# Half of the softmax tiles leave TensorE's transposes for the DMA queue, and the normalisation moves from the tiles to the sums

## The reference

```
g     = x·w_g + b_g          theta = x·w_theta + b_theta      phi = x·w_phi + b_phi
att   = softmax(theta phi, axis=-1)          # 1024 x 1024 for each image
y     = att g                                # 1024 x 64
out   = x + batchnorm(y·w_out + b_out)       # fixed mean, var, gamma, beta
```

## Time and profile before

| | |
|---|---|
| median of 3 runs | 225.07 us (224.91 to 227.15) |
| profiled execution | 224.65 us |
| its span | 222.8 us |
| outside the span | 1.85 us |
| busy: PE, DVE, ACT, POOL | 214.5, 183.9, 169.8, 148.6 us |
| DMA share of the main queue | 31.6% |

### The profile page before, as it was taken

One profiled execution on the slowest core, in us unless ns is written; L12 is line 12 of the kernel. 1 busy time (PEld: TensorE's weight loads), 2 busy tenths in 40 slices (PEclk: granted clock), 3 DMA queues, 4 the chain that ended last, 5 costly groups with the idle time before them and its releaser, 6 DMA issues.

```text
span 222.8 us, 4289 instructions
## 1 busy us (share of the span) xinstructions
PE 214.5 (96%) x1228; PEld 141.5 (63%) x1228; DVE 183.9 (83%) x328; ACT 169.8 (76%) x311; POOL 148.6 (67%) x143
## 2 busy tenths in 40 slices
PE   7997889999999999999999999999999999999994
PEld 6684748656665767657676666647686566656552
DVE  0789998779988699779997799797997799898761
ACT  2687977869688787869698687878878696868751
POOL 2647977786787577966787687866777843843420
PEclk9999999999999999999999999999999999999999
DMA  5107330365106531185104551085200751010102
GB/s 159 72 0 200 79 100 3 108 177 141 47 4 195 135 99 49 43 236 145 47 0 140 151 133 47 0 231 153 61 27 1 188 141 47 0 47 0 50 0 94
DMA packets 8716, 19.78 MB, mean 89 GB/s; under 512 B 1536, under 2 KB 2048, under 8 KB 8704
## 3 DMA queue, kind: packets, MB, share of 16 engines
q1 hardware_dynamic: 8416, 19.50, 31.6%
q10 hardware_dynamic: 288, 0.14, 0.2%
HBM read 4.43 MB, written 4.19 MB: 39 GB/s over the span
## 4 chain that ended last, share of the span: by engine, by line
PE 85%; DVE 6%; DMA 4%; ACT 1%; POOL 1%; issue 0%; SPq 0%; ACTq 0%; DVEq 0%
PE ps_flip L663 25%; PE ps_scores L601 25%; PE ps_y L616 12%; PE ps_y L620 8%; PE ps_misc L628 6%; PE ps_misc L687 4%; PE ps_misc L702 3%; DVE neg_max L496 2%; DMA phi_ll<-lo 2%; DMA vec<-vectors_dram 2%; DVE pt_lo L566 1%; PE ps_misc L607 1%; PE ps_misc L709 1%; DVE phi_ll L484 1%; DVE g_parts L550 1%; ACT L403 1%
## 5 line engine op out<-in xcount | busy, mean ns | idle before, releaser
L316 POOL TENSOR_SCALAR probs<-probs,inv_sum 128x1024 f32<-128x1024 f32 x64 | 72.2, 1127 | 58.3 <-DVE inv_sum L518 58.2
L566 DVE SCALAR_TENSOR_TENSOR pt_lo<-ps_flip,pt_hi 128x512 f16<-128x512 f32 x128 | 82.2, 684 | 25.3 <-ACT pt_hi L446 24.3
L446 ACT ACTIVATE pt_hi<-ps_flip 128x512 f16<-128x512 f32 x128 | 69.7, 597 | 31.6 <-PE ps_flip L663 31.5
L496 DVE TENSOR_REDUCE neg_max<-ps_scores 128x1 f32<-128x1024 f32 x64 | 77.7, 1214 | 0.6 <-PE ps_scores L601 0.5
L663 PEld LDWEIGHTS ps_flip<-ident,probs 128*128 128x128 f32 x512 | 56.9, 141 | 24.7 <-issue 10.3
L455 ACT ACTIVATE probs<-ps_scores,neg_max 128x1024 f32<-128x1024 f32 x64 | 71.8, 1122 | 0.0
L663 PE MATMUL ps_flip<-ident,probs 128*128 128x128 f32 x512 | 68.4, 277 | 3.4 <-POOL probs L316 1.6
L601 PE MATMUL ps_scores<-phi_hh,theta_hl 128*128 128x512 f32 x128 | 45.5, 436 | 0.5 <-DVE phi_ll L484 0.3
L601 PE MATMUL ps_scores<-phi_ll,theta_hl 128*128 128x512 f32 x128 | 40.1, 394 | 0.0
L616 PE MATMUL ps_y<-pt_hi,g_parts 128*128 128x512 f16 (+1 forms) x128 | 32.7, 378 | 0.0
L601 PEld LDWEIGHTS ps_scores<-phi_ll,theta_hl 128*128 128x128 f32 x128 | 24.1, 188 | 5.6
(11 more groups left out here) (77 smaller groups left out, 159.6 us busy)
## 6 DMA issues: line engine op xcount, KB each, us to landing
x_in<-x_in_dram SPq DMA_DIRECT2D x16, 256.0 KB, 3.1
out_dram<-resid SPq DMA_DIRECT2D x15, 256.0 KB, 2.0
phi_hh<-hi SPq DMA_DIRECT2D x14, 256.0 KB, 4.4
phi_ll<-lo SPq DMA_DIRECT2D x14, 256.0 KB, 4.0
theta_hl<-hi SPq DMA_DIRECT2D x7, 256.0 KB, 3.4
theta_hl<-lo SPq DMA_DIRECT2D x7, 256.0 KB, 3.1
out_dram<-resid SPq DMA_DIRECT2D x1, 192.0 KB, 2.0
w_tp<-w_tp_t_dram ACTq DMA_DIRECT2D x1, 128.0 KB, 3.4
```

The costliest lines, as they stand in the source:

```text
L316: nc.gpsimd.tensor_scalar(out=p[:, :], in0=p[:, :], scalar1=inv_sum[:, at:at + 1], scalar2=1.0, op0=ALU.mult, op1=ALU.mult).then_inc(probs ...
L446: nc.scalar.activation(pt_hi[ring][:, c * HALF_TILES:(c + 1) * HALF_TILES, slot * P:(slot + 1) * P], ps_flip[c][:, :].rearrange("p (a n) - ...
L496: nc.vector.tensor_reduce(out=neg_max[:, k % STEPS:k % STEPS + 1], in_=ps_scores[k % 2][:, :], op=ALU.max, axis=AX.X, negate=True).then_in ...
L566: nc.vector.scalar_tensor_tensor(out=pt_lo[ring][where], in0=ps_flip[c][:, :].rearrange("p (a n) -> p a n", n=P), scalar=PROB_SCALE, in1=p ...
```

## The change

No tile but those of the last half is multiplied by its reciprocal sum any more. In every other half, the tiles in slots 0 and 2 of four (`BY_DMA`) are not transposed on TensorE: ScalarE writes an fp16 copy `p_hi` of `probs` right behind the exp, GpSimd subtracts it from `probs` into `p_lo`, and SP issues a transposing DMA for each (`turn_hi`, `turn_lo`) that lands in `pt_hi` and `pt_lo`. The scale 2^15 that TensorE's tiles get from `pt_hi` is put into those tiles' exp, by adding its logarithm to the negated maximum (a small operation of VectorE behind the row maximum), and taken into their reciprocals. The tiles in slots 1 and 3 go as before, without the scaling on GpSimd. The four reciprocals of a half are taken at once, written to DRAM as a row (`inv_to_row`), read back to all 128 partitions (`inv_to_all`), and VectorE multiplies the finished sum by them (`scale_y`, before on ScalarE). SP's loop is written out. In `image`, the lines left out below are the waits and `load_x`, then the three restacks of `hi`, then those of `lo`; the last line of the diff stands ahead of a half's weighted sum.

```diff
+    BY_DMA = (0, 2)
+            def turn_hi(t):
+                if not by_dma(0, t):
+                    return
+                ring, slot = ring_of(t), t % HALF_TILES
+                wait(sp, y_ready, t // HALF_TILES - 1)
+                sp.wait_ge(p_hi_ready, move_at(0, t) + 1)
+                sp.dma_start_transpose(pt_hi[ring][:, :, slot * P:(slot + 1) * P],
+                                       p_hi[ring][BY_DMA.index(slot)][:, :]).then_inc(pt_moved[ring], 16)
+            def turn_lo(t):
...
+            def inv_to_row(h):
...
+                sp.dma_start(inv_row[h % 2].rearrange("(t p) -> p t", p=P),
+                             inv_sum[:, at:at + HALF_TILES],
+                             allow_slow_non_contiguous=True).then_inc(inv_in_row, 16)
+            def inv_to_all(h):
...
+                sp.dma_start(inv_all[h % 2][:, :],
+                             inv_row[h % 2].unsqueeze(0).to_broadcast([P, BANK])).then_inc(inv_spread[h % 2], 16)
             def image(it, k):
                 b, r = image_at(it, k), (k // MT) % 2
+                turn_lo(MT * b - 2)
+                inv_to_row(2 * b - 1)
                 store(it, k - 2 * MT + HALF_TILES)
+                turn_hi(MT * b)
 ...
+                turn_lo(MT * b)
 ...
+                inv_to_all(2 * b - 1)
+                turn_hi(MT * b + 2)
                 store(it, k - MT)
+                turn_lo(MT * b + 2)
 ...
+                inv_to_row(2 * b)
+                turn_hi(MT * b + 4)
+                turn_lo(MT * b + 4)
+                inv_to_all(2 * b)
+                turn_hi(MT * b + 6)
@@ GpSimd, in place of the scaling
+                    hold(pt_moved[ring], moved_by(it, k - 1) - MOVED)
+                    hold(p_hi_ready, move_at(it, k - 1) + 1)
+                    nc.gpsimd.tensor_tensor(low[:, :], p[:, :], high[:, :], ALU.subtract).then_inc(p_lo_ready, 1)
@@ ScalarE, behind the exp of such a tile
+                        act.wait_ge(probs_ready, t + 1)
+                        wait(act, pt_moved[ring_of(k)], moved_by(it, k) - MOVED)
+                        nc.scalar.activation(high[:, :], probs[k % PROB_RING][:, :], ACT.Copy).then_inc(p_hi_ready, 1)
@@ VectorE
+                if by_dma(it, k):
+                    dve.wait_ge(row_max_ready, move_at(it, k) + 1)
+                    nc.vector.tensor_scalar(out=top, in0=top, scalar1=LOG_SCALE, scalar2=None,
+                                            op0=ALU.add).then_inc(max_ready, 1)
+            def scale_y(h, half, r, image, spread):
+                dve.wait_ge(y_unit_ready, image + 1)
+                dve.wait_ge(inv_spread[half], spread)
+                dve.wait_ge(y_ready, h + 1)
+                nc.vector.scalar_tensor_tensor(out=y_norm[:, :], in0=ps_y[:, :], scalar=y_unit[:, r:r + 1],
+                                               in1=inv_all[half][:, :], op0=ALU.mult,
+                                               op1=ALU.mult).then_inc(y_scaled, 1)
@@ TensorE
-                if exists(t, TILES):
-                    pe.wait_ge(probs_scaled, t + 1)
+                if exists(t, TILES) and not by_dma(it, k - 2):
+...
+                        pe.wait_ge(pt_moved[ring_of(k - 6)], moved_by(it, k - 6))
```

More of the change, by code:

```diff
@@ L56, in build_nonlocal_attention @@
     WARM_UP = 6
+    BY_DMA = (0, 2)
+    BY_PE = tuple(slot for slot in range(HALF_TILES) if slot not in BY_DMA)
+    MOVED = 32 * len(BY_DMA)
+    LOG_SCALE = math.log(PROB_SCALE)
+    LAST_HALF = TILES - HALF_TILES
     LAST_PIECES = (slice(0, BANK - P), slice(BANK - P, BANK))
@@ L117, in build_nonlocal_attention @@
         y_norm = sbuf("y_norm", [P, BANK], F32)
+        inv_row = [nc.dram_tensor(f"inv_row{i}", (BANK,), F32).ap() for i in range(2)]
+        p_hi = [[sbuf(f"p_hi{i}{s}", [P, N], F16) for s in BY_DMA] for i in range(2)]
+        p_lo = [[sbuf(f"p_lo{i}{s}", [P, N], F16) for s in BY_DMA] for i in range(2)]
+        inv_all = [sbuf(f"inv_all{i}", [P, BANK], F32) for i in range(2)]
         ps_scores = [psum(f"ps_scores{i}", [P, N]) for i in range(2)]
@@ L176, in build_nonlocal_attention @@
         inv_sum_ready = sem("inv_sum_ready")
+        inv_raw_ready = sem("inv_raw_ready")
+        inv_in_row = sem("inv_in_row")
+        row_max_ready = sem("row_max_ready")
+        p_hi_ready = sem("p_hi_ready")
+        p_lo_ready = sem("p_lo_ready")
+        pt_moved = [sem(f"pt_moved{i}") for i in range(2)]
+        inv_spread = [sem(f"inv_spread{i}") for i in range(2)]
         probs_scaled = sem("probs_scaled")
@@ L204, in tile_is, with in_last_half, by_dma, flip_at @@
             return isinstance(it, int) and tile_at(it, k) == t
+        def in_last_half(t):
+            return isinstance(t, int) and t >= LAST_HALF
+        def by_dma(it, k):
+            return k % HALF_TILES in BY_DMA and not in_last_half(tile_at(it, k))
+        def flip_at(it, k):
+            if in_last_half(tile_at(it, k)):
+                return LAST_HALF // HALF_TILES * len(BY_PE) + tile_at(it, k) - LAST_HALF
+            before = sum(slot < k % HALF_TILES for slot in BY_PE)
+            return it * (STEPS // HALF_TILES * len(BY_PE)) + k // HALF_TILES * len(BY_PE) + before
+        def move_at(it, k):
+            before = sum(slot < k % HALF_TILES for slot in BY_DMA)
+            return it * (STEPS // HALF_TILES * len(BY_DMA)) + k // HALF_TILES * len(BY_DMA) + before
+        def moved_by(it, k):
+            return it * (STEPS // HALF_TILES // 2 * MOVED) + (k // HALF_TILES // 2 + 1) * MOVED
+        def ring_of(k):
+            return k // HALF_TILES % 2
         def is_first(image):
@@ L271, in image @@
                     restack(phi_ll[1 - r], CI, lo, CI, 1 - r)
-            image(0, 0)
-            image(0, MT)
-            with sp.Fori(1, B // 2 - 1) as it:
+                inv_to_row(2 * b)
[3 more added lines that the diff above has]
+                turn_hi(MT * b + 6)
+            for it in range(B // 2):
                 image(it, 0)
                 image(it, MT)
-            image(B // 2 - 1, 0)
-            image(B // 2 - 1, MT)
             store(B // 2, -2 * MT + HALF_TILES)
@@ L453, in step @@
                     act.wait_ge(max_ready, t + 1)
-                    wait(act, flipped, 2 * (t - PROB_RING) + 2)
+                    if by_dma(it, k - PROB_RING):
+                        wait(act, p_lo_ready, move_at(it, k - PROB_RING) + 1)
+                    else:
+                        wait(act, flipped, 2 * flip_at(it, k - PROB_RING) + 2)
                     nc.scalar.activation(probs[k % PROB_RING][:, :], ps_scores[k % 2][:, :], ACT.Exp,
@@ L654, in step @@
                 t = tile_at(it, k - 2)
-                if exists(t, TILES):
-                    pe.wait_ge(probs_scaled, t + 1)
+                if exists(t, TILES) and not by_dma(it, k - 2):
+                    f = flip_at(it, k - 2)
+                    if in_last_half(t):
+                        pe.wait_ge(probs_scaled, t - LAST_HALF + 1)
+                    else:
+                        pe.wait_ge(probs_ready, t + 1)
                     for c in range(2):
-                        if isinstance(t, int) and t == 0:
+                        if isinstance(f, int) and f == 0:
                             pe.wait_ge(*((g_out, 1), (shift_ready, 1))[c])
-                        wait(pe, pt_lo_ready, 2 * t + c - 1)
+                        wait(pe, pt_lo_ready, 2 * f + c - 1)
                         for a in range(HALF_TILES):
```

81 lines of the change are left out of this document (58 added, 23 removed).

## The result

The changed kernel takes 324.93 us (321.08 to 326.59, 4 runs), the one before 224.99 us beside it: the ratio is 1.4347, 95% interval 1.4215 to 1.4478. The forecast was 216, at most 250. The profiled execution took 321.08 us, its span is 319.2 us.

A forecast was written before the change was run, and what follows sets the result against it. TensorE was taken as the bound: span 222.8 - 25.2 + 7 + 8 + about 1 = 213.6 us, plus 1.85 outside = 215.5, median 0.4 higher, so 216 us. Likeliest case 208 to 222; whole range 204 to 250.

The forecast's parts named there:

- the one sentence on the row of reciprocals: SP's queue after a half's last tile: two small DMAs of 2 to 4.4 us each fit in some 8 us.
- The last line of the prediction: Signs of being wrong: transposes landing in over 6 us, PE waiting for pt_lo or pt_moved, or late small reciprocal DMAs.
- TensorE, removed: On TensorE, the transposes of two tiles in each of 15 halves go: 30 x 0.84 = 25.2 us.
- The other engines keep up: ACT, DVE and POOL at 19.6, about 20 and about 20 us an image fit the 22.2 us of an image.
- rival 2: Other engines set the pace: two score buffers, each pair of tiles loses 0.3 us, 222 to 228 us; chance 0.09.
- `scale_y` has lost its cover: Ahead of the output convolution, PE waits 0.1 to 0.8 us for the scaled sum; 0.5 on 14 halves, 7 us.
- SP's queue: 14 transfers ahead of the next image's scores take 14.9 us; a wait of 1.2 in 7 images, 8 us.
- the third, slow transposes: On SP's queue ahead of the lo restacks, slow transposes make DMA the bound: slower than before, 233 to 267 us; chance 0.28.

The follow-up runs named there:

- experiment 6: Changed kernel, every tile transposed by TensorE; 512-piece rows of reciprocals written but nobody waiting for them, the spread reading a row of x: 247.93 us, 1.1023.
- experiment 4: Changed kernel with no tile on the DMA queue: all transposed by TensorE, the rows of reciprocals kept: 252.01 us, 1.1229 to the kernel before.
- experiment 5: Changed kernel with all tiles transposed by TensorE, and the row written in 128 pieces of 16 bytes instead of 512 of 4: 226.83 us, 1.0083.
- experiment 7: Changed kernel, slots 0 and 2 still by DMA, with the row in 16-byte pieces and scale_y reading at a stride: 237.98 us, 1.0581.
- experiment 9: Changed kernel with the row in 16-byte pieces and only the tile in slot 0 of each half by DMA: 234.87 us, 1.0469.
- experiment 3: Changed kernel with its transposes, without the reciprocals' DMAs and the waits for them, scale_y taking a constant: 233.57 and 237.15 us.
- experiment 8: Changed kernel with plain copies in 256-byte pieces for the transposes, and no rows, scale_y taking a constant: 234.75 us, 1.0437.
- experiment 13: Changed kernel with 16-byte pieces, slots 0 and 2 by DMA; in steps ending a half's sum, its second part precedes that step's scores: 231.32 us, 1.0302.
- experiment 10: Changed kernel with the row in 16-byte pieces and only the tile in slot 2 of each half by DMA: 219.09 us, 0.9745.

## Why the prediction was wrong

**The step that failed** is the one sentence on the row of reciprocals: "two small DMAs after the last tile of the half, 2 to 4.4 us each, against three steps, some 8 us and more. That is enough, unless the queue below is late." The range came from transfers of 256 KB, as if fewer bytes could only be quicker. This transfer has four-byte pieces, and took 8.3 us alone, 9.3 in the middle among other traffic and 12.5 in the changed kernel. I had bounded a piece's price only from the share of the engines' time (25 ns a packet), and the share stays at 3% while the row is under way: that view could not show it. The diff did show the pieces, with `allow_slow_non_contiguous` beside them. The Trainium skill says that pieces under 512 bytes fall short of the line rate, since the engine reads and modifies what it writes (DMA: Bandwidth & Descriptors, Specifications); both forms of the row are under that, so that alone does not tell them apart; here they are 512 pieces of four bytes and 128 of 16, with 9.3 and 2.6 us. In its place the runs showed two effects: what is issued behind the row lands after it (experiment 6: 23 us with nobody waiting), and with the transposes in the same queue the loss is 324.9 - 238.0 = 87 us instead of 252.0 - 226.8 = 25 (experiments 4, 5, 7). That the two together are more than their sum is measured; that it is because more of each image's chain stands behind each row fits the timeline, but was not isolated. The last line of the prediction had named late small DMAs as what would make it wrong, and gave that no price and no chance.

**TensorE, removed:** 240 transposes fewer, x272 instead of x512. Slot 2 alone gains 5.65 us of the 15 x 0.84 = 12.6. The other 7 us are idle time (11.5 in all) and PE's busy time, which is 205.5 where 214.5 - 12.6 = 201.9 was due.

**The other engines keep up:** right, or nearly, in every size that was not in the trace of before: `p_hi` 1.06 us (taken 1.0), `p_lo` 2.13 (2.3 to 2.56, so a little under), the small addition 0.15 (0.15), `scale_y` 0.75 (0.73). The sum had nothing for waits for an exp, which only rival 2 priced: they are 5.2 us in experiment 7 and 7.5 in 9.

**`scale_y` has lost its cover:** right in kind, too high in size. With the operation at the forecast's length and no row in the way the wait is 1.9 us in seven waits of up to 0.6 (experiments 3 and 8), against 7 in waits of 0.1 to 0.8. The 7.2 us of experiment 7 match by luck, 5.5 of them being the stride. In the changed kernel itself the term can't be seen, as the wait for the row covers it.

**SP's queue:** right in place, low in size: 15.5 us in seven waits of 2.2 against 1.2 each. The term that was off is the length of the burst, 17.9 instead of 14.9 us. A transpose costs 1.38 us of the engines, and SP is occupied 13.8 us by the 14 issues, which alone is over my 13.3 of engine time; a transpose holds it 1.2 us or more, where a plain issue had 0.46.

**The clock** was in no term. PE's busy time in experiment 7 is 202.4 us where 189.3 was due, 13.1 us, and the same instructions took 195.2 in experiment 13 at a higher mean clock. Not all of the 13.1 is the clock, as the 3.6 us of experiment 10 at 1.00 show. With that, 213.6 + 6.5 (restacks) + 0.2 (`y_norm`) + 13.1 + 5.2 (waits for an exp) - 2.4 (small waits that fell) give the 236.2 us of span. A forecast that had priced the row rightly and no more would still have been 20 us low.

**The rivals:** the third, slow transposes, ended on the right side for a reason that was not its own. At 1.4 us a transpose it put the time at about 227, and experiments 3 and 8 agree on 235 with either form. The trace does not bear out the Trainium skill's 1309 ns for one 128x128 block by DMA (VectorE: DVE Perf Modes, The three transpose paths) as a price in a row: eight blocks in one transfer cost 1.38 us together. The Trainium skill's 261 GB/s (DMA: Bandwidth & Descriptors, Latency and other measured facts) would be an estimated 1.0 us; the measured burst has 161 / 0.85 = 190 GB/s, and the measurement decides.

## What to carry to other kernels

Price a small DMA by its number of pieces as well as its bytes, and ask what is queued behind it: a slow one delays transfers that have nothing to do with it. When a resource's share is high, read the bytes moved in the same stretch before calling it bandwidth. And before work is moved off the engine that sets the pace, ask what that work was hiding: of two equal tiles, the one whose transposes covered nothing made the kernel 2.5% faster, the other made it 4.7% slower (part of that because the scaling it exposes had itself become slower). And when an experiment's edit also changes an operation, read that operation's length again before a wait is put down to the forecast.

## What the hardware showed that was not expected

- A write of 2 KB from 128 partitions to DRAM: 512 pieces of four bytes land in 8.3 us alone (11.0 and 11.6 for two issued together) and 9.3 among other traffic, 128 pieces of 16 bytes in 2.6 among other traffic, with the engines busy 3 to 4% in the first case.
- Transfers issued right behind such a row on the same queue: three stores took 11.5 to 12.5 us instead of 2.0, and spreads 10.8 in the median instead of 3.2.
- The same VectorE operation over 512 columns took 1.14 us with one input read at a stride of four elements, 0.75 without.
- In the changed kernel the main queue's packets took 0.927 x 319.2 = 296 us of 16 engines for 39.2 MB, and with 16-byte pieces 0.788 x 236.2 = 186 us for the same bytes: the share grows with time spent behind the row, so it is no measure of the load.
- A transposing DMA of 128x1024 fp16 costs a quarter more than the same copy in 256-byte pieces (1.38 and 1.10 us), and occupies the issuing queue 1.33 us.
- After an idle PE of 8.34 us the granted clock was 0.50, and eight transposes took 1.92 us instead of 1.04. Behind shorter waits both are seen: 0.58 after 2.39 us in experiment 8 (145.5 to 149 us), 1.00 after 2.47 us in experiment 7 (117 to 120). What decides there stays open.
